# Linear attention with a routed FFN: an earlier state update, keys before queries, logits behind the sums, gate rows from SBUF

## What is computed

```python
h = layernorm(x) * (1 + ca) + sa
q, k, v = phi(h @ Wq), phi(h @ Wk), h @ Wv          # 16 heads of 16, phi = elu + 1
S += k_t v_t^T ; z += k_t ; out_t = (S^T q_t) / max(z . q_t, eps)   # causal scan over a sequence
x = x + ga * (out @ w_out)
h = layernorm(x) * (1 + cb) + sb
gates = softmax(h @ w_router)                        # 8 experts, top 2, capacity 1280 rows each
x = x + gb * sum_e combine[:, e] * (silu(h @ w_gate) @ w_down[e])
```

## Time and profile before

| | us |
|---|---|
| median of 3 runs | 929.94 (926.96 to 939.68) |
| the profiled execution | 929.81 |
| its span, first to last instruction | 928.1 |

### The profile page before, as it was taken

One profiled execution on the slowest core, in us unless ns is written; L12 is line 12 of the kernel. 1 busy time (PEld: TensorE's weight loads), 2 busy tenths in 40 slices (PEclk: granted clock), 3 DMA queues, 4 the chain that ended last, 5 costly groups with the idle time before them and its releaser, 6 DMA issues.

```text
span 928.1 us, 35097 instructions
## 1 busy us (share of the span) xinstructions
PE 783.3 (84%) x14631; PEld 674.0 (73%) x14631; DVE 552.2 (60%) x1805; ACT 487.2 (52%) x941; POOL 482.0 (52%) x621
## 2 busy tenths in 40 slices
PE   6786778798888868798988787967799999999994
PEld 4565656576666666576766666755799999999994
DVE  5564456566657656465765664654175776677762
ACT  4554455555565654466656556543165555545551
POOL 2103125545645546365655474545546676667664
PEclk9999989989999989899999999997899999999997
DMA  5489721222323223232221231224347766776663
GB/s 181 162 244 269 225 48 55 86 82 83 107 70 93 107 56 97 59 94 97 72 68 69 42 71 44 42 53 72 117 108 161 157 138 138 161 147 135 136 111 40
DMA packets 71467, 99.69 MB, mean 107 GB/s; under 512 B 7810, under 2 KB 52866, under 8 KB 71320
## 3 DMA queue, kind: packets, MB, share of 16 engines
q1 hardware_dynamic: 38744, 53.93, 21.6%
q0 software_dynamic: 21760, 31.66, 15.1%
q10 hardware_dynamic: 10816, 11.96, 4.3%
HBM read 46.84 MB, written 63.36 MB: 119 GB/s over the span
## 4 chain that ended last, share of the span: by engine, by line
PE 70%; issue 11%; DVE 10%; POOL 4%; DMA 2%; ACT 1%; SPq 0%; POOLq 0%; ACTq 0%; DVEq 0%
PE SCW L1704 12%; PE SCW L1719 6%; PE SCW L1389 6%; PE PM L1422 5%; PE PJ L1475 4%; PE SB L1446 4%; PE SCW L1343 4%; PE SCW L1374 4%; PE PM L1475 4%; DVE Sm L975 3%; PE PM L1434 3%; PE PM L1719 3%; PE SB L1719 3%; PE PM L1485 3%; DVE KT L1023 2%
## 5 line engine op out<-in xcount | busy, mean ns | idle before, releaser
L507 POOL DMA_INDIRECT slot_rows<-Hrow,sloti x128 | 129.2, 1010 | 132.1 <-PE SCW L1389 71.3
L623 POOL DMA_INDIRECT out<-EX,desti x80 | 125.1, 1564 | 24.9 <-POOL idle L453 11.8
L975 DVE TENSOR_TENSOR Sm<-SCW,tri 128x1024 f32<-128x1024 f32 x64 | 78.0, 1219 | 35.4 <-PE SCW L1343 29.4
L453 POOL TENSOR_TENSOR idle<-mhalf 128x1 f32<-128x1 f32 x136 | 59.3, 436 | 71.4 <-DVE EX L1273 44.3
L1446 PE MATMUL SB<-w_og,AK 128*128 128x256 f32 x256 | 78.5, 431 | 17.3 <-issue 14.4
L1005 DVE TENSOR_TENSOR Snew<-PM,headmask 128x136 f32<-128x136 f32 x64 | 19.2, 299 | 115.3 <-PE PM L1422 115.3
L557 POOL TENSOR_TENSOR hT<-N,hT 128x512 fp32r<-128x512 f32 x30 | 38.2, 1273 | 73.1 <-ACT hT L676 72.4
L1389 PE MATMUL SCW<-Sm,VA 64*17 64x64 f32 x4096 | 60.6, 220 | 13.7 <-issue 13.7
L839 ACT ACTIVATE OTs<-SCW 128x512 f32<-128x512 f32 x64 | 38.3, 598 | 58.8 <-PE SCW L1389 58.8
L691 ACT ACTIVATE N<-X,nb,rs 128x256 f32<-128x256 f32 x128 | 66.2, 589 | 5.2 <-POOL nb L567 4.7
L876 ACT ACTIVATE VA<-SCW 128x512 f32<-128x512 f32 x80 | 48.0, 599 | 39.3 <-PE SCW L1704 38.6
(11 more groups left out here) (250 smaller groups left out, 2057.9 us busy)
## 6 DMA issues: line engine op xcount, KB each, us to landing
Hrow<-slot_rows SPq DMA_DIRECT2D x32, 516.0 KB
slot_rows<-erow ACTq DMA_DIRECT2D x1, 10400.0 KB, 45.8
X<-x SPq DMA_DIRECT2D x16, 512.0 KB, 4.6
out<-X SPq DMA_DIRECT2D x16, 512.0 KB
Hrow<-mod_rows SPq DMA_DIRECT2D x16, 512.0 KB
QT<-slot_rows SPq DMA_DIRECT2D x8, 516.0 KB
slot_rows<-Hrow,sloti POOLq DMA_INDIRECT x128
N<-wd SPq DMA_DIRECT2D x4, 512.0 KB
```

What stands on the lines that cost most here:

```text
L453: pool.tensor_tensor(idle[:, k:k + 1], mhalf[:, 0:1], mhalf[:, 0:1], ALU.add).then_inc(breath, 1)
L507: pool.indirect_dma_start(xe, bass.IndirectOffsetOnAxis(sloti[:, par, k, t:t + 1], 0), Hrow[:, par, t, :], None, bounds_check=last_slot, o ...
L623: pool.indirect_dma_start(out, bass.IndirectOffsetOnAxis(desti[s % 2][:, a:a + 1], 0), Ys[s % 2][:, a, :], None, bounds_check=TOK - 1, oob ...
L975: dve.tensor_tensor(Smh(T % 2), SCW[:, :, 0:2 * P].rearrange("p r (m i) -> p r m i", i=CH), tri64[:].unsqueeze(1).unsqueeze(1).to_broadcas ...
```

## The change

Four edits, none of which adds a computation or leaves one out.

- **Gate rows.** MB gets a fourth row, the gate row, so its load is 4 x 4 x 256 values a partition instead of 4 x 3 x 256. The gate values in Hrow come from MB by an SBUF to SBUF DMA, and only for the first two groups of a sequence (one for each half of Hrow), 8 times in all. SP's loop over groups is unrolled, and starts when MB is there.
- **State update.** add_to_state stands between from_state and from_tile in all slots.
- **Keys ahead.** m = 0 and 1 are now the keys, m = 2 and 3 the queries. columns_and_keys waits for the group's first two phis, and stands ahead of the value projection in slot 3 too.
- **Logits.** They follow from_tile in slot 0 and go to PJ[0]; the transposes of the first half go to PJ[1], the out product follows, then the second half goes to PJ[0] once lgT is copied. ScalarE copies lgT behind OTs. logit_rows moves ahead of columns_and_keys in slot 1, and take with it. hT_raw lies in a free part of Sm instead of in N1.

```diff
@@ -37,6 +37,7 @@
 TPB = SEQ // P
+GPB = TPB // GT
 E = 8
@@ -90,7 +91,7 @@
         saca2 = sb("saca2", [P, 2 * DC])
-        MB = sb("MB", [P, BATCH, 3, D])
+        MB = sb("MB", [P, BATCH, 4, D])
         ident = sb("ident", [P, P])
@@ -163,7 +164,7 @@
         w_g_raw = h2T[:]
-        hT_raw = N1[:].rearrange("p t d -> p (t d)").rearrange("p (c n) -> p c n", c=DC)
+        hT_raw = Smf[:, 3 * DC * GW:4 * DC * GW].rearrange("p (c n) -> p c n", c=DC)
         VAf = VA[:].rearrange("p a t h w -> p (a t h w)")
@@ -326,6 +327,10 @@
+        def lgt_of(g):
+
+            return PJ[1 if g == GROUPS - 2 else 0][:, 0:P]
+
         def part(k):
@@ -349,7 +354,7 @@
             sp.dma_start(MB[:].rearrange("p b k d -> p b (k d)"),
-                         mod_rows[:, 0:3 * D].unsqueeze(0).to_broadcast([P, BATCH, 3 * D])).then_inc(mb_in, 16)
+                         mod_rows.unsqueeze(0).to_broadcast([P, BATCH, 4 * D])).then_inc(mb_in, 16)
@@ -358,22 +363,20 @@
-            def leave(i, k):
-                g = i * 2 + k
+            def leave(g):
+                k = g % 2
                 sp.wait_ge(x1_done, g * GT + GT)
-                sp.dma_start(out[bass.ds(g * GW, GW), :].rearrange("(t p) d -> p t d", p=P),
-                             X[:, bass.ds(g * GT, GT), :]).then_inc(stored, 16)
-                at_least(sp, sent[k], i * 128)
-                sp.dma_start(Hrow[:, k, :, D + 4:ROW],
-                             mod_rows[bass.ds(i // 2, 1), 3 * D:4 * D].unsqueeze(1).to_broadcast([P, GT, D])
-                             ).then_inc(gb_in[k], 16)
+                sp.dma_start(out[g * GW:(g + 1) * GW, :].rearrange("(t p) d -> p t d", p=P),
+                             X[:, g * GT:(g + 1) * GT, :]).then_inc(stored, 16)
+                if g % GPB < 2:
+                    at_least(sp, sent[k], g // 2 * 128)
+                    sp.dma_start(Hrow[:, k, :, D + 4:ROW],
+                                 MB[:, g // GPB, 3, :].unsqueeze(1).to_broadcast([P, GT, D])).then_inc(gb_in[k], 16)
             sp.wait_ge(w_lo, 1)
-            for k in range(2):
-                leave(0, k)
-            with sp.Fori(1, GROUPS // 2) as i:
-                for k in range(2):
-                    leave(i, k)
+            sp.wait_ge(mb_in, 32)
+            for g in range(GROUPS):
+                leave(g)
             def load_wd(ep, k, n):
@@ -461,7 +464,7 @@
                     at_least(pool, rested, g)
-                    pool.wait_ge(gb_in[g % 2], 16 * (g // 2 + 1))
+                    pool.wait_ge(gb_in[g % 2], 16 * (g // GPB + 1))
                     pool.wait_ge(route, NR * g + NR)
@@ -665,9 +668,10 @@
                 N = G + 1
-                act.wait_ge(pj_full, 8 * N + 2)
+                act.wait_ge(pj_full, 8 * N + cidx + 1)
+                at_least(act, h_lo, 2 * (N - 1) + cidx + 1)
                 b = N // 4
-                act.activation(hT_raw[:, cidx, :], PJ[cidx][:], ACT.Identity, scale=saca[:, DC + cidx, b:b + 1],
+                act.activation(hT_raw[:, cidx, :], PJ[1 - cidx][:], ACT.Identity, scale=saca[:, DC + cidx, b:b + 1],
                                bias=saca[:, cidx, b:b + 1]).then_inc(h_raw, 1)
@@ -683,7 +687,7 @@
                     act.wait_ge(av_done, 4 * (N - 1))
-                dst = QT if m < 2 else KT
+                dst = KT if m < 2 else QT
                 act.activation(EX[:, m % 2, :], PJ[m % 2][:], ACT.Exp)
@@ -703,7 +707,7 @@
                 act.wait_ge(rstd2, GROUPS - 1 + (1 if t < GT - 1 else 2))
-                act.wait_ge(h_lo, 2 * GROUPS)
+                act.wait_ge(pj_full, 8 * (GROUPS - 1) + 2)
                 normalise(N1[:, t, :], t, (GROUPS - 1) * GT + t, rs2, nb2, n2_ready)
@@ -754,9 +758,14 @@
-                    act.wait_ge(h_lo, 2 * L)
+                    act.wait_ge(pj_full, 8 * (L - 1) + 2)
                 for t in range(GT):
                     normalise(N1[:, t, :], t, L * GT + t, rs1, nb1, n1_ready)
+
+            def logits_kept(g):
+
+                act.wait_ge(lgt_full, g + 1)
+                act.activation(lgT[:], lgt_of(g), ACT.Copy).then_inc(lgt_done, 1)
@@ -801,10 +810,11 @@
                 routed = group_ok(g)
+                if n == TILES - 1:
+                    logits_kept(g)
                 if routed and step in ("first", "pick"):
-                    act.wait_ge(lgt_full, g + 1)
-                    act.activation(lgT[:], PJ[1][:, 0:P], ACT.Copy).then_inc(lgt_done, 1)
-                if n >= -1 and q != 3:
+                    take(lg, lg_ps[:, :, 0:E], lg_full, g)
+                if n >= -1:
                     columns_and_keys(n)
@@ -821,10 +831,6 @@
                         stage1_v(G, 0, npar, nx)
-                if n >= -1 and q == 3:
-                    columns_and_keys(n)
-                if routed and step in ("first", "pick"):
-                    take(lg, lg_ps[:, :, 0:E], lg_full, g)
                 if n == TILES - 2:
@@ -838,6 +844,8 @@
                                    ).then_inc(ot_done, 1)
+                if routed and step == "columns":
+                    logits_kept(g)
                 if stage1 and q == 0:
@@ -1018,7 +1026,7 @@
                 N = G + 1
-                dst = (QT if m < 2 else KT)[:, npar, m % 2, :]
+                dst = (KT if m < 2 else QT)[:, npar, m % 2, :]
                 dve.wait_ge(pj_read, 6 * N + m + 1)
@@ -1355,7 +1363,7 @@
                     t = n + 1
-                    pe.wait_ge(phi_done, 4 * (t // 4) + 4)
+                    pe.wait_ge(phi_done, 4 * (t // 4) + 2)
                     at_least(pe, ak_done, n + 1)
@@ -1446,18 +1454,20 @@
-            def stage1_transposes(G, gn):
+            def stage1_transposes(G, gn, cidx):
                 N = G + 1
-                pe.wait_ge(n1_ready, 4 * N + 4)
-                at_least(pe, pj_read, 6 * N)
-                if group_ok(gn - 2):
-                    pe.wait_ge(h2t_done, 2 * (G - 2) + 2)
-                if G >= 0:
-                    pe.wait_ge(state_read, 4 * G + 2)
-                for cc in range(DC):
-                    for t in range(GT):
-                        last = pe.transpose(PJ[cc][:, t * P:(t + 1) * P], N1[:, t, cc * P:(cc + 1) * P], ident[:])
-                    last.then_inc(pj_full, 1)
+                if cidx == 0:
+                    pe.wait_ge(n1_ready, 4 * N + 4)
+                    at_least(pe, pj_read, 6 * N)
+                    if group_ok(gn - 2):
+                        pe.wait_ge(h2t_done, 2 * (G - 2) + 2)
+                    if G >= 0:
+                        pe.wait_ge(state_read, 4 * G + 2)
+                elif group_ok(gn - 2):
+                    pe.wait_ge(lgt_done, G - 2 + 1)
+                for t in range(GT):
+                    last = pe.transpose(PJ[1 - cidx][:, t * P:(t + 1) * P], N1[:, t, cidx * P:(cidx + 1) * P], ident[:])
+                last.then_inc(pj_full, 1)
@@ -1472,7 +1482,7 @@
                     for cc in range(DC):
-                        last = mm(PJ[m % 2][:], w_qkv[:, wp, cc, m * P:(m + 1) * P], hT[:, hp, cc, :],
+                        last = mm(PJ[m % 2][:], w_qkv[:, wp, cc, (m + 2) % 4 * P:((m + 2) % 4 + 1) * P], hT[:, hp, cc, :],
                                   start=(cc + i == 0), stop=(cc == DC - 1 and i == len(SPLIT) - 1))
@@ -1517,21 +1527,22 @@
-            def logits(g, gn, stage1):
-
-                pe.wait_ge(state_read, min(4 * gn + 2, TILES))
-                if stage1:
-                    pe.wait_ge(h_raw, 2 * (gn + 1) + 2)
+            def logits(g):
+
+                if g == GROUPS - 2:
+                    pe.wait_ge(state_read, TILES)
                 pe.wait_ge(h2t_done, 2 * g + 2)
                     for t in range(GT):
-                        last = mm(PJ[1][32 * t:32 * t + 32, 0:P], w_r[:, cc, :], h2T[:, cc, t * P:(t + 1) * P],
+                        last = mm(lgt_of(g)[32 * t:32 * t + 32, :], w_r[:, cc, :], h2T[:, cc, t * P:(t + 1) * P],
                                   start=(cc == 0), stop=(cc == DC - 1), skip_group_check=True)
-            def logit_rows(g):
+            def logit_rows(g, gn):
                 pe.wait_ge(lgt_done, g + 1)
+                if group_ok(gn + 1):
+                    pe.wait_ge(h_raw, 2 * (gn + 1) + 1)
                 pe.transpose(PJ[1][:, P:2 * P], lgT[:], ident[:]).then_inc(lg_full, 1)
@@ -1611,7 +1622,9 @@
-                if n >= -1 and q != 3:
+                if routed and step in ("first", "pick"):
+                    logit_rows(g, gn)
+                if n >= -1:
                     columns_and_keys(n)
@@ -1624,10 +1637,6 @@
                         stage1_v(G, 0)
-                if n >= -1 and q == 3:
-                    columns_and_keys(n)
-                if routed and step in ("first", "pick"):
-                    logit_rows(g)
                 if routed and step == "place":
@@ -1637,19 +1646,21 @@
                     from_state(n)
-                if n >= -1 and tile_ok(n + 1) and q == 0:
+                if n >= -1 and tile_ok(n + 1):
```

(12 more changed lines are left out.)

## The result

| | us |
|---|---|
| after, median of 4 runs | 878.19 (875.24 to 884.01) |
| before, beside it, median of 4 | 932.51 (926.96 to 939.68) |
| ratio | 0.942, 95% interval 0.934 to 0.951 |
| the profiled execution of after, its span | 875.24, 873.5 |

Between the two profiled executions the time fell by 54.6 us. The page of after has this for its clock (40 slices) and its instruction queue; the windows are those of the earlier trace rows, cut where the stages now change.

A forecast was written before the change was run, and what follows sets the result against it. PE was taken to run out of instructions in the slots, the fetch held behind slow gate-row loads. -45.6 + 2 - 17.2 - 7.1 + 3 = -64.9 from 929.81 gave 865 us, own range 852 to 876, wider range 843 to 903.

The forecast's parts named there:

- rival 2: The eight gate loads that stay still hold the fetch, or pauses move to row sends and stores: 879 us, chance 0.12.
- rival 1: VectorE stuck behind POOL's row send after all, so head columns come late and PE waits at columns_and_keys: 883 us, chance 0.17.
- Gate rows, -45.6: Last slots of groups: 31.6 us go with the dropped loads, 11 at three kept loads, 3 at group 14's.
- the loads that stay: Kept gate loads, now from SBUF, run at the store's rate: 4 of 14.9 us excess stay, 11 go (bounds 0 and 15).
- MB's load, +2: MB's load, ahead of the first gate rows, grows from 1536 to 2048 KB: +2 us, all on the path.
- State update, -17.2: Snew runs under from_tile's 64 matmuls, ahead of POOL's row send, so PE's 17.2 us of waits for it go.
- Keys ahead of queries, -7.1: columns_and_keys of slot 3 no longer waits for the group's fourth phi: PE's 7.1 us of waits go.
- Logits, 0: Slot 0: the wait before the logits (11.0 us) goes, but the chain behind decides, so 0; bounds -11 and +2.
- More pauses, +3: PE draws the same instructions in less time, so pauses that no gate load causes grow: +3 us, bounds 0 and 10.
- Rival 3: The gate load is not what starves PE, so only the waits go: 908 us, chance 0.06.
- rival 4: More gain: the logits' 11 us come too and fewer half-clock stretches give some 7: 847 us, chance 0.10.
- rival 5: Slower: every send of slots 1 and 2 (78) holds VectorE 1.40 us on the path: 974 us, chance 0.03.

The follow-up runs named there:

- e1: The kernel before with the gate-row edit alone (eight loads from MB, the three order edits left out): 891.70 us, 0.959 of the kernel before.
- e3: The kernel before with one edit, add_to_state between from_state and from_tile in all four slots: 909.63 us, 0.981 of the kernel before.
- e5: The changed kernel with all sixteen gate-row loads, each from MB in SBUF: 859.40 us, 0.967 of the kernel before on the second chip.
- e10: The changed kernel with the logits, the halves and their waits as before: 861.23 us, 0.964 of the kernel before on the third chip.
- e2: The changed kernel with the gate-row edit undone (sixteen loads from DRAM) and the three order edits kept: 912.71 us, 0.980 of the kernel before.
- the changed kernel again: The changed kernel, nothing altered, measured a second time on the third chip: 864.09 us, 0.966 of the kernel before.

## Why the prediction was right

865 us was forecast and 878 measured, inside the range of 843 to 903. It is 2 us outside the forecast's own range (852 to 876), and the number alone fits rival 2 (879) and rival 1 (883) better. What tells them apart is the traces and e1, e3 and e5. The signs named for the forecast came: the pauses fell from 60.0 to 34.6 us, the last slots have a median of 7.71 us, the group shown takes 31.23, Snew is on time, and the transposes of An wait at most 0.5 us in a slot. By the profiled executions the sum was -64.9 us, and 54.6 came. Step by step:

**Gate rows, -45.6.** The mechanism held: most of the long pauses went, the last slots came down (93.8 us for 133.2 over groups 3 to 14), and e1 gives 38 us, a little under the 43.6 of this term with MB's. The guess for the loads that stay was sound: they run at the store's rate and land in 3.3 and 4.0 us (the loads of 230 and 115 us); one of the eight has a pause soon after it (1.95 us, to 122.85). Rival 2 falls with that, and e5 agrees: eight more such loads cost nothing that can be seen. That a pause costs more than its length is seen in before too: behind the one of the earlier trace rows, from 334.20 to 337.00 us, the granted clock is 0.50. In the profile of e1 the first expert matmul comes at 628.62 us for 670.60, 42.0 less by the trace, all but the forecast's 43.6; the rest of its time is the experts' (below).

**MB's load, +2.** Little is seen of it: the wait for w_og is 2.8 us in after and 4.0 in e1, 2.9 before.

**State update, -17.2.** e3 gives 17.6 (8 to 27), and in after Snew starts 0.04 to 0.24 us after its matmuls in every slot. Rival 1 falls on the first chip: in e3 the transposes of An wait 1.9 us in all and in after 4.5 (1.8 before), not 18 more. Two steps were incomplete. The claim that add_to_state's waits are "long met" missed one, for ScalarE's copy of the router rows (7.7 us in e3 and in e10); in the changed kernel it is hidden because the logits edit moves that copy forward. And the 1.40 us were taken for a property of the kernel, where the second chip had 0.3.

**Keys ahead of queries, -7.1.** The wait went. The transposes of An wait 2.7 us more in after, but not for this edit: e10, which has it, waits 2.5 us for An, and 5.5 come with the logits edit. No run had this edit alone; e2 beside e3 says only that it and the logits edit together are within 3 us of nothing, with intervals of 10.

**Logits, 0.** Right in the sum, and for the reason given: PE arrives earlier and waits, from_state for the mask 12.4 us. Mis-sized inside it was the push. It was taken to be what the split of the halves brings back; it is 0.81 us a group more than nothing, 10 us in 13 groups, and only because 19.6 us of waits go does the edit come out even.

**More pauses, +3.** Where no gate load stands, in the first three slots of groups 3 to 14, what lies above the median of each place sums to 17.0 us, 15.2 before: +1.8. For the first place alone it is +3.5 (11.5 for 8.0).

**Outside the sum.** The experts were put at no change. They took 4.3 us more, and the change edits nothing there: from the first matmul of a gate product to the last matmul of the stage it is 245.0 us in before and 249.3 in after, and 244.9 to 255.7 over the fourteen profiled executions, with code that is the same in all. These are 4 of the 10 us by which the sum missed, and they are scatter. The first expert matmul of after comes 58.9 us earlier (611.72), where the two halves in e1 and e2 brought 42.0 and 24.4 (646.19), 66.4 together against the forecast's 67.9 without the +3. That they agree so well is in part luck: e3, with the 17.2 us edit alone, comes 28.3 us earlier (642.26), more than all three order edits in e2, so one execution is good to some 10 us. The 6 to 8 us that are missing in the whole are of the size by which executions of one kernel scatter (875 to 884 us for after). No run pins them to a step.

**Rival 3** (908 us) falls by e1, **rival 4** (847 us) and **rival 5** (974 us) by the time. Of rival 5, sends holding VectorE where its work has moved beside them, not one slot is seen in after.

On the rule of the Trainium skill that the prediction cited beside rows 8 (SBUF — State Buffer, the list under the diagram): on the first chip Snew, with one input in PSUM, stood until the send was over, which that clause doesn't foresee, and on the second it ran in the middle of the send, which agrees with it, as do the additions to X inside the sends of e3. What the depth of PE's buffer in rival 3 would make (the Trainium skill, Runtime: NRT & Kernel Launch, Instruction fetch mechanics) is not borne out: PE stands still after 252 to 419 matmuls and weight loads behind the last landing, and e1 shows that the pauses, and most of the gain, follow the loads.

## What to carry to other kernels

When an engine stands still and no other engine owes it anything, look at what the DMA queues move in those microseconds, and at the rate: a small broadcast that read one row of DRAM over and over moved at less than a quarter of the store's rate here, and with the rows taken from SBUF it moved at that rate. An instruction packet can be what stands behind it. Before moving work forward on an engine, follow the longest chain that starts behind it; the waits that vanished in the list here (19.6 us) bought nothing that could be measured, since the moved work itself pushed that chain back. And measure on more than one chip before giving a wait of an engine a price: the change was worth 5.8% in the result and 3.4% on the third chip.

## What the runs showed of the hardware that I had not expected

- **One row, 80 GB/s.** 512 KB read as 512 copies of one 1 KB row of DRAM move at 80 to 90 GB/s; the same 512 KB from 128 rows of DRAM peak at 379 GB/s, and from SBUF at 363.
- **An instruction packet starts when the slow load ends.** In 57 of 57 slow loads the next packet of queue 8 starts between 1.4 us before and 0.7 us after the load's end, though it moves in about 1 us once it has started. Between 60 and 560 us before takes up to 12.2 us from one packet's start to the next, e1 up to 9.2 and after up to 8.7.
- **Chips differ in one wait.** The kernel before takes 931, 893 and 898 us on three chips, with scatter of 1% to 2% on each. A part of the difference is in the slots with a send: Snew 1.40 us late on one, 0.30 to 0.35 on another, with identical instructions; as PE waits for it 21 times on the first chip and never on the other, that is up to 17 of some 35 us. PE shows a trace of the same: on the first chip it pauses inside add_to_state in the third slot of 12 groups (0.24 to 0.34 us each in e2 and after), with the second send's end just before. In the profiles of the changed kernel and e5 on the other two chips no third slot has this pause. The third slot has a median of 7.71 us in after, and 7.16 in e5 and in the changed kernel on the other two. Each set was made on one chip at one time, so chip and time can't be told apart, and what differs isn't known from these runs.
- **Pauses without a load.** Besides the wait ahead of the logits, 20 to 35 us of "issue" waits stay in every kernel here that has the quick loads, those over 1 us most often at from_tile and logits and up to 5.0 us long. The three over 2 us in after that stand between matmuls of one line end 1.3 to 1.5 us after the landing of an instruction packet as well, with no slow load in the kernel. They fall in other groups in each profile (243, 320 and 377 us in after; 207, 313 and 479 in the changed kernel again), and kernels without one slow load still scatter by 1%.
